# Recommender scoring kernel: an earlier and split weight burst, evacuation ahead of the splits, and four gathered rows of tile 1 summed on TensorE

## The reference

```
retrieved   = mean(item_embeddings[indices], axis=1)          # 512 x 512
fused_rep   = concat([user_rep, retrieved]) @ W_fuse + b_fuse # 512 x 512
logits      = fused_rep @ W_proj + b_proj                     # 512 x 12500
```

## Time and profile before

| | |
|---|---|
| median of three runs | 338.95 us (338.04 to 339.5) |
| the profiled execution | 338.66 us |
| its span | 336.6 us (2.06 us lie around it) |
| TensorE matmul busy | 318.3 us, 95% |
| VectorE, GpSimd, ScalarE busy | 184.9, 82.3, 68.5 us |
| DMA | 75.24 MB, mean 224 GB/s |

### The profile page before, as it was taken

One profiled execution on the slowest core, in us unless ns is written; L12 is line 12 of the kernel. 1 busy time (PEld: TensorE's weight loads), 2 busy tenths in 40 slices (PEclk: granted clock), 3 DMA queues, 4 the chain that ended last, 5 costly groups with the idle time before them and its releaser, 6 DMA issues.

```text
span 336.6 us, 4239 instructions
## 1 busy us (share of the span) xinstructions
PE 318.3 (95%) x1464; PEld 260.9 (78%) x1464; DVE 184.9 (55%) x317; ACT 68.5 (20%) x102; POOL 82.3 (24%) x84
## 2 busy tenths in 40 slices
PE   4959998599999999999999999999999999999996
PEld 1429876498888898888888888888888888888884
DVE  5899598795678833625454444535354544435222
ACT  2330653530020024022022220222012221020000
POOL 4777778677777100000000000000000000000000
PEclk9996999999999999999999999999999999999999
DMA  7994998989997212786755776568757466442222
GB/s 277 363 396 93 414 383 246 323 270 402 376 338 210 96 62 98 176 333 248 213 162 216 230 243 185 176 249 244 201 161 249 181 213 213 161 166 99 91 91 91
DMA packets 33837, 75.24 MB, mean 224 GB/s; under 512 B 5686, under 2 KB 21830, under 8 KB 33824
## 3 DMA queue, kind: packets, MB, share of 16 engines
q1 hardware_dynamic: 26912, 60.11, 52.2%
q0 software_dynamic: 6336, 13.92, 12.6%
q10 hardware_dynamic: 576, 1.05, 0.8%
HBM read 55.47 MB, written 25.60 MB: 241 GB/s over the span
## 4 chain that ended last, share of the span: by engine, by line
PE 71%; DVE 0%; issue 0%
PE bank L660 69%; PE bank L646 2%; PE bank L636 0%; DVE total L471 0%; DVE out_sb L535 0%
## 5 line engine op out<-in xcount | busy, mean ns | idle before, releaser
L660 PE MATMUL bank<-w_hi,f_hi 128*128 (+1 forms) x400 | 155.8, 390 | 0.0
L660 PE MATMUL bank<-w_lo,f_hi 128*128 (+1 forms) x400 | 155.3, 388 | 0.0
L660 PE MATMUL bank<-w_hi,f_lo 128*128 (+1 forms) x400 | 155.1, 388 | 0.0
L535 DVE TENSOR_TENSOR out_sb<-bank,early 128x500 f32<-128x500 f32 x92 | 62.4, 678 | 128.1 <-PE bank L660 125.5
L660 PEld LDWEIGHTS bank<-w_hi,f_lo 128*128 128x128 f32 x400 | 75.1, 188 | 15.5
L660 PEld LDWEIGHTS bank<-w_hi,f_hi 128*128 128x128 f32 x400 | 75.2, 188 | 15.0
L660 PEld LDWEIGHTS bank<-w_lo,f_hi 128*128 128x128 f32 x400 | 75.2, 188 | 15.0
L327 ACT CAST w_hi<-w_raw 128x1000 fp32r<-128x1000 f32 x46 | 47.1, 1029 | 151.4 <-DMA w_raw<-w_proj 96.4
L267 POOL DMA_INDIRECT ring<-item_embeddings,rows x68 | 71.0, 1045 | 24.8 <-issue 16.6
L507 DVE TENSOR_TENSOR w_lo<-w_raw,w_hi 128x1000 fp32r<-128x1000 f32 (+1 forms) x58 | 55.4, 977 | 2.3 <-ACT w_hi L327 2.3
L471 DVE SCALAR_TENSOR_TENSOR bank<-ring,mask,bank 128x512 f32<-128x512 f32 x56 | 42.1, 752 | 4.5 <-DMA ring<-item_embeddings,rows 1.0
(11 more groups left out here) (60 smaller groups left out, 61.6 us busy)
## 6 DMA issues: line engine op xcount, KB each, us to landing
logits<-out_sb SPq DMA_DIRECT2D x100, 250.0 KB, 2.6
w_raw<-w_proj SPq DMA_DIRECT2D x46, 500.0 KB, 6.9
early<-b_proj SPq DMA_DIRECT2D x25, 250.0 KB, 5.9
early<-w_proj SPq DMA_DIRECT2D x4, 500.0 KB, 6.7
ring<-item_embeddings,rows POOLq DMA_INDIRECT x68, 6.2
early<-user_t ACTq DMA_DIRECT2D x4, 256.0 KB, 4.1
early<-w_fuse SPq DMA_DIRECT2D x4, 256.0 KB, 5.4
wf_ret<-w_fuse SPq DMA_DIRECT2D x1, 1024.0 KB, 19.0
```

Source lines behind the costliest of these rows:

```text
L535: nc.vector.tensor_tensor(out_sb[:, g % OUT_SLOTS, :], ps[:, 0:CHUNK], bias[:, c % BIAS_SLOTS, 0:CHUNK], ALU.add).then_inc(evacuated, 1)
L660: m = nc.tensor.matmul(ps[:, 0:CHUNK].unsqueeze(1), f[:, t, k, :], w, start=begin, stop=(f is f_lo and k == HK - 1))
```

## The change

Five things are altered.

1. SP waits for tile 0's slot 12 (`BURST_AT`) in place of slot 16, and then issues chunks 2 and 3 alone. Chunks 4 and 5 wait for f of tile 0 (`f_hi_ready`).
2. Chunks 6 and 7 land in `early` (the buffers of chunks 2 and 3) in place of `w_raw`, and are issued behind the stores of groups 0 and 1. The bias broadcasts, which use the same memory, go behind the stores of groups 6 and 7, four each.
3. ScalarE evacuates groups 0 to 3 ahead of `split_hi` of chunks 4 to 7, and group 6 ahead of `mean(1)`.
4. `PE_LAST` is 4: TensorE adds slots 13 to 16 of tile 1, VectorE thirteen, and `home`, added last, writes the finished sum (`home_last`).
5. The turn stands behind group 6, and `fuse` in the middle of group 7. VectorE takes the bias remainder (`bias_lo`) and the count of laps two additions later.

```diff
-PE_LAST = 2
+BURST_AT = 12
+PE_LAST = 4
...
         def raw_of(c):
-            return c if c < 4 else c % 2
+            return c % 4 if c < RESIDENT else c % 2
...
-            sp.wait_ge(slot_landed[place(0, PASSING - 1)], 16 * slot_uses(0, PASSING - 1))
-            for c in range(2, 6):
-                load_chunk(c)
+            sp.wait_ge(slot_landed[place(0, BURST_AT)], 16 * slot_uses(0, BURST_AT))
+            load_chunk(2)
+            load_chunk(3)
+            sp.wait_ge(f_hi_ready, HK)
+            load_chunk(4)
+            load_chunk(5)
             for c in range(RESIDENT):
+                store(0, c)
                 if c < 2:
                     load_chunk(c + 6)
-                store(0, c)
-                if c == RESIDENT - 3:
-                    sp.wait_ge(lo_ready, 8)
-                if c >= RESIDENT - 3:
-                    for b in range(3 * (c - RESIDENT + 3), min(3 * (c - RESIDENT + 4), BIAS_SLOTS)):
+                if c >= RESIDENT - 2:
+                    sp.wait_ge(lo_ready, 2 * c + 2)
+                    for b in range(4 * (c - RESIDENT + 2), 4 * (c - RESIDENT + 3)):
                         load_bias(b)
...
             for c in range(RESIDENT):
-                if c < 2:
-                    split_hi(c + 4)
-                if c == RESIDENT - 2:
+                if c == RESIDENT - 1:
                     mean(1)
-                if c == RESIDENT - 1:
                     fused_hi(1)
                 evacuate_first(c)
                 if c < PE_LAST:
                     keep_last(c)
-                if c in (2, 3):
+                if c < 4:
                     split_hi(c + 4)
...
+            def home_last(t):
+                return last_add(t) <= HOME_AFTER
...
-                nc.vector.tensor_tensor(total_ps[:] if t else total[:], total_ps[:], home[:], ALU.add).then_inc(home_added, 1)
+                final = t == 0 or home_last(t)
+                if t and final:
+                    dve.wait_ge(ret_turned, t)
+                nc.vector.tensor_tensor(total[:] if final else total_ps[:], total_ps[:], home[:], ALU.add)\
+                  .then_inc(home_added, 1)
...
                     if halfway is not None and k == HK // 2:
-                        turn_sum(halfway)
+                        fuse(halfway)
...
-                    halfway = t + 1 if c == RESIDENT - 2 and t + 1 < TILES else None
-                    project_resident(t, c, halfway)
-                    if halfway is not None:
-                        fuse(halfway)
+                    project_resident(t, c, t + 1 if c == RESIDENT - 1 and t + 1 < TILES else None)
+                    if c == RESIDENT - 2 and t + 1 < TILES:
+                        turn_sum(t + 1)
```

More of the change, by code:

```diff
@@ L153, in raw_of @@
         def raw_of(c):
-            return c if c < 4 else c % 2
+            return c % 4 if c < RESIDENT else c % 2
         def raw_uses(c):
-            return 1 if c < 4 else c // 2
+            return c // 4 + 1 if c < RESIDENT else (c - RESIDENT) // 2 + 3
         def place(t, i):
@@ L192, in load_chunk @@
                     if c >= 4:
-                        sp.wait_ge(lo_ready, 2 * (c - 4 if c < 6 else c - 2) + h + 1)
+                        sp.wait_ge(lo_ready, 2 * (c - 4 if c < RESIDENT + 2 else c - 2) + h + 1)
                     sp.dma_start(raws[raw_of(c)][:, 2 * h:2 * h + 2, :], w_proj[c, :, 2 * h:2 * h + 2, :])\
@@ L468, in add @@
                     dve.wait_ge(added, adds_done(t, i - 1))
-                if i == last_add(t):
+                final = i == last_add(t) and not home_last(t)
+                if final:
                     dve.wait_ge(ret_turned, t)
-                nc.vector.scalar_tensor_tensor(total[:] if i == last_add(t) else total_ps[:], here,
+                nc.vector.scalar_tensor_tensor(total[:] if final else total_ps[:], here,
                                                mask[:, t, i + 1:i + 2], total_ps[:], ALU.mult, ALU.add).then_inc(added, 1)
@@ L480, in add_last @@
                     return
-                if t == 1:
-                    dve.wait_ge(home_added, 1)
+                if t == 1 or home_last(t - 1):
+                    dve.wait_ge(home_added, t)
                 else:
@@ L550, in _ @@
             sort(3)
-            for i in range(5):
+            for i in range(7):
                 add(0, i)
             count_columns()
-            bias_lo()
-            add(0, 5)
-            add(0, 6)
             split_lo(0, (0,))
@@ L559, in _ @@
             add(0, 8)
+            bias_lo()
             split_lo(0, (1,))
@@ L630, in turn_sum @@
                         sum_in(ring[:, place(1, i), :], ret_t[:, j, :], first=(j == 0), ps=turn_bank(1))
-                    pe.wait_ge(added, adds_done(1, last_add(1)))
+                    pe.wait_ge(home_added, 2)
                     sum_in(total[:], ident[:], last=True, ps=turn_bank(1)).then_inc(ret_turned, 1)
```

## The result

The changed kernel took 345.99 us (median of 344.75, 345.48, 346.49 and 347.78); the kernel before, run beside it, 339.23 (338.04 to 339.63). The ratio is 1.0209, with a 95% interval of 1.0155 to 1.0264: slower, where 335.8 us had been forecast, in a range of 334.2 to 338.3. The profiled execution took 344.75 us, its span is 342.7, against 338.66 and 336.6 before.

What follows compares the result with a forecast made beforehand. TensorE's unbroken run of matmuls to the end was taken as the bound, with 6.2 us lost ahead of it. -4.9 + 1.86 + 0.2 = -2.9 us from 338.66 gave 335.8, range 334.2 to 338.3.

Steps and rivals of the forecast that it cites:

- -4.9 us: Tile 0's groups: the three TensorE stalls go, and 1.3 of the 6.2 us lost there stay.
- for order, not for throughput: TensorE's three waits ahead of tile 1: evacuations sat behind splits and stores in the order; supply was not the limit.
- 2.4 us per half chunk: W loads of chunks 4 to 7: time per half chunk at some 210 GB/s left beside the gathers.
- late next: VectorE at group 6 of tile 0: its split_lo of chunk 6 makes TensorE wait 0.8 us.
- +1.86: Tile 1's turn: two more slots summed on TensorE cost 1.86 us, all on the path.
- I take 3.5 us and no move: Burst behind slot 12 of tile 0: late slots take 3.5 us to land, and f does not move.
- nearer to the quiet row: Slots meeting the burst: only two do, so latency lies nearer 2.1 us than the 5.9 to 7.9 under W traffic.
- "0" for the count: Count of laps some 1.6 us later in tile 0: costs 0, as TensorE stands 4.42 us for slot 11 anyway.
- +0.2: Tile 2's sum: ready at 91.5, 1.5 us earlier; TensorE waits 0.6 where it waited 0.41, so +0.2 us.
- rival A: Tile 2's gathers do not move, its sum stays at 93.04, only 1.36 us is gained: 337.3; chance 0.10.
- I take 0: Turn behind group 6, fuse in the middle of group 7: costs 0, at most 1 us if f_lo is late.
- Rival C: Tile 0's sum: burst delays slots 14 to 16, f 2.6 late, clock low for 3.3 more: 341.7; chance 0.09.

Runs made afterwards that it cites:

- the causes removed: The kernel of the order alone with PE_LAST = 4, so four slots on TensorE; bursts, count and turn as before: 340.21 us, ratio 1.0038.
- the burst alone: Kernel before with only chunks 2 and 3 issued behind slot 12, chunks 4 and 5 still behind slot 16: 340.93 us, ratio 1.0106.
- the order alone: Kernel before with only the new order of evacuations, splits, stores and chunks 6 and 7; two slots on TensorE, turn as before: 338.53 us, ratio 1.001.
- the ladder: Table adding parts to the kernel before: order 1.001, four slots 1.0038, burst split with f's wait and late count 1.014, turn behind group 6 1.0209.

## Why the prediction was wrong, step by step

- **"-4.9 us" for the three stalls: failed.** This is the term that the forecast rested on. In the changed kernel the stage from group 0 to tile 1 is 32.56 us, as forecast, but with group 0 at 38 it is 35.34 with the change's own order on TensorE (burst behind 16, old count), 38.07 with four slots and the turn in the middle of group 6, and 36.20 with two slots. Against 35.96 before, and with 1.86 for two more slots taken off, the best of these shows 2.5 of the 4.9. As far as the traces show, the stalls went in the changed kernel because its groups came 6.6 to 7.1 us later than in those kernels while the last half of chunk 7 was split only about 3 us later (63.67 for 60.08 to 60.86). The step called the waits "for order, not for throughput" because of a split that had waited 4.58 us, and estimated 2.4 us per half chunk. But with 2.4 us per half, four chunks are 19 us: issued from 39.8, with its 2 us to the first bytes, the last half lands at about 61. It was split at 60.86 in the first of these kernels, and evacuation 4 behind it let the turn begin at 62.41, which the forecast had near 60.7. The estimate held and was not carried to chunk 7. Its "late next" (VectorE, group 6) was right for the changed kernel: 0.65 us for `w_lo`.
- **"+1.86" for two more slots: undersized.** The matmuls took what was said where the clock stayed up. What the sum had too small was their other effect: the buffers they hold keep GpSimd from tile 2's slots (3.34 us in the changed kernel, 4.37 with the causes removed). The part on tile 2's sum knew of that wait, had the turn's end at 65.3 and slot 7 at 67.9; they came at 70.7 and 74.38. Price: about 1.7 us between the two kernels of one chip.
- **"I take 3.5 us and no move" for the burst: failed.** The slots took 3.7 to 6.2 us with the burst alone and 6.2 to 7.3 with the count, and f was 3.2 or 5.1 late, counted from the first gather. The choice "nearer to the quiet row" had no ground: the row of 2.1 us was of a stretch with a DMA share of 0.08, and the burst fills just that stretch. The Trainium skill, "DMA: Bandwidth & Descriptors", section "Queues, rings and completion order", spoke against this part. The direction of its estimate held, and its size (slots up to 5 us later) is near the 3.3 to 4.5 us by which slots 13 to 16 landed later after their issue than before; no run shows that whole packets were the reason. (The estimate's 2.5 us per packet goes with the 413 GB/s of the earlier trace rows, not with the 210 that it names.)
- **"0" for the count: failed.** TensorE's wait for slot 11 hid it from TensorE, but GpSimd issues the lap and slots 13 to 16 behind it: slot 13 goes 1.45 us later, and group 0 comes 1.9 us later than with the burst alone.
- **"+0.2" at tile 2's sum: failed**, and here rival A (tile 2's gathers do not move) was right in its mechanism: with the order alone the sum is at 93.31 where it was 93.04, and takes back whatever was gained ahead. With the whole change it came at 96.98, where 91.5 was expected.
- **"I take 0" for the turn's place: failed**, and no rival named the way. The step priced `f_lo` at the group behind the fuse; that needed nothing, as its 0 said. The loss was at group 7, now directly behind the turn, whose bank waits for evacuation 5 and that for a store: 2.2 us.
- **Rival C** had the right place and kind: f late, the clock at 0.50 in its stead. Its price of +5.9 less the gain of 2.9 gave 341.7; what it lacked is that the gain hardly exists without its own delay, and the loss at the turn. It had 0.09, and the range left it out.

What stays open: the late count was timed alone only at the high level, and the wait for f ahead of chunk 4 nowhere; in the ladder both stand in one row with the burst, so the 1.0% of that row is not divided by times. The row of the change without the early burst and the late count (1.0131) is dearer than its turn of tile 2 (93.44) says; its trace of 339.77 us was among the fastest of its eight executions (339.58 to 344.21), and what the slower ones did differently has no trace.

## What to carry to other kernels

A stall that names an engine's place in the order may only be the last link of a late supply: before pricing it as order, lay the landings of the whole stream beside the times at which they are needed, to the last piece. Ask at the next point where two chains meet (here the sum of tile 2) how much slack the other one has; if it is 0.4 us, a gain ahead is worth 0.4 us. And quiet time on the DMA engines may be quiet because a chain of small transfers is running there, each waited for: here filling it with bulk made that chain late.

## What the runs showed of the hardware that was not expected

- Gathers of few rows took 2.1 to 3.1 us on near-empty DMA engines and 6.2 to 7.3 beside loads of 500 KB (DMA share 0.99, 373 GB/s in 32 to 38).
- A store of 250 KB issued behind four loads of 500 KB on one queue landed after 9.8 us, its like in the kernel before after 10.3; over the changed kernel the median of a store is 2.7.
- The length of TensorE's stand does not by itself say whether its clock falls. The granted clock went from 1.00 to 0.50 after 2.66 us (order alone) and 2.27 us (four slots) ahead of tile 1's turn, and the matmuls behind took 3.37 us for 2.02. It also fell after only 1.68 us in the changed kernel (behind a wait of 0.60 us ahead of the four matmuls of the turn). It stayed at 1.00 after 2.04 us in the kernel with the burst alone (ahead of group 6) and after 1.95 us, behind one of 0.73, with burst and count undone.
- The same program took 338 us on some chips and 355 to 359 on others. There the mean granted clock is 0.95 to 0.99 for 0.98 to 1.00, and single waits of 5 to 8 us appear for which no releaser is recorded.
